# Spare expert tiles on pads, the first batch's text turned first, router logits between weight chunks, early expert tiles behind fewer scatters

## The chip, the cores and the metric

One NeuronCore of a Trainium2 chip runs the whole program as one launch. The metric is device time in microseconds (us), median of the runs; an execution taken by the hardware profiler gives the trace. Engines: TensorE (PE, its weight loads PEld), VectorE (DVE), ScalarE (ACT), GpSimd (POOL) and SyncE (SP); the last issues most DMAs.

## The reference, cut to what matters

```python
h = _L0_tok_ref(log_dt, inv_A_real, A_imag, B_ri, x, 256)      # (8, 256, 256): image tokens from a Vandermonde sum
h = jnp.concatenate([h, txt], axis=1)                          # (8, 768, 256): 256 image rows, 512 text rows
h = h + _L0_attn_ref(_layernorm(h), Wq, Wk, Wv, Wo)            # 16 heads, 4 KV heads, rotary, width 64
h = h + _L0_ffn_ref(_layernorm(h), Wr, br, W1, b1, W2, b2)     # mixture of experts

# _L0_ffn_ref, on 6144 tokens xf of width 256, 8 experts, top 2:
logits = xf @ Wr + br
topk_w, topk_idx = jax.lax.top_k(logits, 2)
topk_w = jax.nn.softmax(topk_w, axis=-1)
h_e = relu(xf @ W1[e] + b1[e]);  y_e = h_e @ W2[e] + b2[e]     # 256 -> 512 -> 256
out = sum over the two chosen e of topk_w[e] * y_e
```

Everything is f32. With the given inputs the reference sends 2973, 3193, 593, 370, 1534, 1205, 1973 and 447 token copies to experts 0 to 7 (2616 to expert 0 in the first seven batches).

## The kernel before, in words

The program has four stages, each in blocks of its own; a block starts when every engine has ended the one before.

1. `vandermonde` computes the image rows of all batches on DVE (complex products), PE (L197) and ACT (copies into `kt`, L171). SP loads all inputs at its start, ends with the stores of batch 0's image rows to `img_d` (L143) and waits for them.
2. `attention` has a start for batch 0 and then a loop of 32 iterations (8 batches x 4 KV heads), 24 steps each: PE scores (L656), DVE maximum (L812), ACT exponential (L725), DVE transpose (L818), PE values (L663). In the start SP loads `x` (batch 0: image from `img_d`, L516, text, L517), the rotary table (L612) and stores the other seven batches' image rows (L614). DVE takes the mean and variance of six 128-row tiles (`stats`), a chain of small instructions gives the reciprocal root, POOL normalises tiles 0 and 1 (L781) and DVE tiles 2 to 5 (L850). PE transposes (L633), ACT copies to `xT` (L713), PE projects K then Q in halves of 384 tokens (L642; `FIRST` is the list of these jobs), ACT copies each into `raw`, and `rotate` on DVE (L470 to L475) applies the rotary table to K half 0, K half 1, Q half 0, Q half 1, with `probT` as scratch. SP moves K (`move_k`), then the first four heads of Q (L622), and the scores start. `probT` lies where `kt` was, so DVE waits for the image stores first.
3. `route` runs over 8 batches of six tiles. PE projects each tile with `Wo` (`project`, L980: eight chunks, so 16 instructions); after tile 1 it transposes the batch before (L988), after tile 2 it computes that batch's router logits (`logits`, L996: 24 instructions with 8 output columns each), after tile 3 its counts (L1003, L1004). DVE adds the residual, normalises, picks the two experts (`choose`) and the rows of the sorted table `xs_d` (`place`); POOL scatters the rows there (L963, twelve indirect DMAs for a batch, in `scatter`). The sorted table has a region for each expert; after its last row 128 pad rows are written (L934, L1066), with a token number past the end.
4. `experts` runs 103 tiles of 128 sorted rows (`NT`), since that many can be needed. `tile_table` on DVE computes the expert (`exp_i`) and first row (`src_i`, L1209) of each tile. SP loads rows (L1258) and `W1` (L1262, 512 KB) four tiles ahead; PE transposes (L1292), goes up (L1302) and down (L1309); DVE adds the bias and gates (L1382, L1384); POOL adds the result to the output with an indirect DMA that accumulates (L1365). Add j waits for the adds j-2 and j-3, and at the first tile of an expert also for j-1 (`adds_i`). Rows whose token number is past the end are not written. Tiles past the last real one read the last real tile again with a gate of zero, and each of them also waits for the add before. SP waits for all scatters and pads (`landed`, L1267) before it loads the first rows.

The order on each engine is that of the program; nothing is planned at run time.

Of the kernel before, what the change touches and what calls it, by code (L numbers as in the profile page):

```python
# [17 lines left out]
P = 128  # L18
NB, SEQ, D = 8, 768, 256
# [15 lines left out]
NT = TOK * TOPK // P + NE - 1  # L35
DX = D + 8
# [37 lines left out]
def vandermonde(nc, sem, io, ident, img_d, wq, wk, wv, wr, br, loaded):  # L74
# [10 lines left out]
    with ExitStack() as ctx:  # L85
# [31 lines left out]
        stored = sem("v_stored")  # L117
        id_ready, known, sq_ready = sem("v_id_ready"), sem("v_known"), sem("v_sq_ready")

        with nc.Block() as block:  # L120
            @block.sync
            def _(sp):
# [15 lines left out]
                sp.dma_start(br[:], io["br"].unsqueeze(0).to_broadcast([P, NE])).then_inc(loaded, 16)  # L138

# [63 lines left out]
            def _(v):  # L203
# [77 lines left out]
                for q in range(4):  # L281
# [11 lines left out]
                    v.wait_ge(g_ready, q + 1)  # L293

# [12 lines left out]
def attention(nc, sem, io, ident, img_d, oT_d, wq, wk, wv, loaded, kt, wo, oT, wo_in, oT_in):  # L307
# [23 lines left out]
    FIRST = N_JOBS + K_JOBS + Q_JOBS + Q_JOBS  # L331
    FIRST_AT = {"n": 0, "k": 3, "q": 7, "q1": 11}
# [9 lines left out]
    ON_POOL = 2  # L342
    NORMS = 2 * TT + 15
    Q_MOVES, K_MOVES, V_MOVES, V_STORES = 4, 4, NQ, NQ
    with ExitStack() as ctx:
# [4 lines left out]
        x, st, mv = sb("a_x", [P, TT, D]), sb("a_st", [P, TT, 6]), sb("a_mv", [P, TT, 2])  # L350
        ve, y, y2 = sb("a_ve", [P, TT]), sb("a_y", [P, TT]), sb("a_y2", [P, TT])
# [19 lines left out]
        table_in, x_in, norm_dve, norm_ready = sem("a_table_in"), sem("a_x_in"), sem("a_norm_dve"), sem("a_norm_ready")  # L371
        x_done, x_out, v_in, set_ready = (sem(f"a_{n}") for n in ("x_done", "x_out", "v_in", "set_ready"))
        q_stored, v_stored, rows_stored = sem("a_q_stored"), sem("a_v_stored"), sem("a_rows_stored")
        q_first, norm_first = [sem(f"a_q_first{j}") for j in range(GH)], sem("a_norm_first")
# [137 lines left out]
        with nc.Block() as block:  # L512
            @block.sync
            def _(sp):
# [49 lines left out]
                def iteration(b, g):  # L564
                    i = b * KV + g
                    if first_it(i):
                        hold(sp, x_done, len(N_JOBS))
                        hold(sp, rows_stored, (NB - 1) * 16)
                        load(1)
# [41 lines left out]
                load(0)  # L611
# [3 lines left out]
                hold(sp, part["k"], 2 * LINKS)  # L615
                move_k(0, 0)
# [9 lines left out]
            def _(pe):  # L626
                def project(X, job, c, h, xn, g):


                    if job == "n":  # L630
# [65 lines left out]
                pe.wait_ge(norm_ready, 1)  # L696
                pe.wait_ge(norm_first, 1)
                pe.wait_ge(loaded, LOADED)
                for n, (job, c, h) in enumerate(FIRST):
                    wait(pe, x_out, len(N_JOBS) if n == len(N_JOBS) else n - NQ + 1)  # L700
# [5 lines left out]
            def _(act):  # L706
                def evacuate(X, n, job, c, h, free):
# [4 lines left out]
                    if job == "n":  # L712
# [22 lines left out]
                def copies(b, g, s):  # L735
                    for bb, gg, n, (job, c, h) in jobs_at(b, g, s):
# [3 lines left out]
                        if job == "k" and h == 0:  # L740
                            free = part["k"], bb * (2 * LINKS) + (c + 1) * LINKS
# [24 lines left out]
                for n, (job, c, h) in enumerate(FIRST):  # L766
                    free = (part["q"], (c + 1) * LINKS) if n >= FIRST_AT["q1"] and h == 0 else None
# [4 lines left out]
            def _(pool):  # L772
                scratch = [prod[:, n, :] for n in range(4)]

                def normalise(n):
                    if n > 0:
# [704 lines left out]
```

## Time and profile before

| | us |
|---|---|
| median of 3 runs | 2267.47 (2265.6 to 2272.73) |
| the profiled execution | 2265.04 |
| span of its trace | 2263.3 |
| mean granted TensorE clock | 0.959 of full speed |

| engine | busy us | share of the span |
|---|---|---|
| PE | 2047.4 | 90% |
| PEld | 1237.6 | 55% |
| DVE | 1770.0 | 78% |
| ACT | 1072.6 | 47% |
| POOL | 879.4 | 39% |

The busy shares are averages over four stages, each with another limit, so they tell little by themselves. In a stage the reader looks for the engine that never rests, and where none is, for the chain of waits. In the rows further down, the brackets at the end of a row give the idle time of that engine before the instruction and what ended it. A granted clock of 1.00 is 2.4 GHz and 0.50 is 1.2 GHz.

### The profile page before, as it was taken

How to read it: one execution, taken by the hardware profiler on the slowest of the kernel's cores; microseconds unless marked ns; L12 is line 12 of the kernel's file. 1: busy time of each engine (PE TensorE's matmuls, PEld its weight loads, DVE VectorE, ACT ScalarE, POOL GpSimd, SP SyncE). 2: the span in 40 equal slices, each digit the busy share in tenths (PEclk: the TensorE clock that was granted, in tenths of full speed). 3: DMA queues.
4: the chain of work that ended last, by engine and by line, in shares of the span. 5: the costliest groups of instructions: out<-in, count | busy, mean ns of one | idle time of the engine just before them, and what ended most of it. 6: DMA issues, size and time to landing. Idle time of an engine off the chain costs nothing. (4 is left out here: it accounts for less than half of the span.)

```text
span 2263.3 us, 59177 instructions
## 1 busy us (share of the span) xinstructions
PE 2047.4 (90%) x21098; PEld 1237.6 (55%) x21099; DVE 1770.0 (78%) x3212; ACT 1072.6 (47%) x2463; POOL 879.4 (39%) x833
## 2 busy tenths in 40 slices
PE   0369999999999999999999999997899949999997
PEld 0234444444444444444444445443588839999996
DVE  8769999999999999999999999999144544444443
ACT  2035655655556555655665565555021114444442
POOL 0023454264344542642444436221034443444443
PEclk6689999999999999999999999999899969999998
DMA  2143543634544445435444453453677648898885
GB/s 51 43 107 90 136 118 92 159 106 103 142 113 126 117 107 137 116 108 128 120 120 120 102 133 105 117 131 95 202 258 269 216 136 212 210 212 209 215 210 117
DMA packets 189542, 317.28 MB, mean 140 GB/s; under 512 B 48661, under 2 KB 127121, under 8 KB 189329
## 3 DMA queue, kind: packets, MB, share of 16 engines
q1 hardware_dynamic: 156640, 275.39, 45.1%
q0 software_dynamic: 19440, 25.83, 6.2%
q10 hardware_dynamic: 13248, 13.13, 1.7%
q8 instruction: 144, 2.36, 0.5%
q14 instruction: 70, 0.57, 0.1%
HBM read 214.75 MB, written 92.31 MB: 136 GB/s over the span
## 5 line engine op out<-in xcount | busy, mean ns | idle before, releaser
L725 ACT ACTIVATE a_prob<-ps_s,a_nmax 128x768 f32<-128x768 f32 x768 | 686.3, 898 | 578.9 <-DVE a_nmax L812 578.9
L812 DVE TENSOR_REDUCE a_nmax<-ps_s 128x1 f32<-128x768 f32 x768 | 694.1, 943 | 49.4 <-PE ps_s L656 44.2
L818 DVE STREAM_TRANSPOSE a_probT<-a_prob 128x768 f32<-128x768 f32 x768 | 700.0, 949 | 1.4 <-PE ps_o L663 1.4
L656 PE MATMUL ps_s<-a_kT,a_qT 64*128 64x384 f32 x3072 | 614.7, 514 | 54.7 <-ACT a_prob L725 50.8
L663 PE MATMUL ps_o<-a_probT,a_vrep 32*64 32x384 f32 x12288 | 561.2, 491 | 6.8 <-DVE a_probT L818 5.0
L656 PEld LDWEIGHTS ps_s<-a_kT,a_qT 64*128 64x128 f32 x3072 | 259.7, 186 | 391.5 <-ACT a_prob L725 275.3
L788 POOL TENSOR_TENSOR a_o<-a_o,a_invrow 128x1536 f32<-128x1536 f32 x32 | 110.0, 3437 | 791.0 <-ACT a_o L733 791.0
L663 PEld LDWEIGHTS ps_o<-a_probT,a_vrep 32*64 32x64 f32 x12288 | 243.6, 132 | 293.8 <-issue 129.9
L470 POOL TENSOR_TENSOR a_prod<-a_raw,a_table 128x384 f32<-128x384 f32 x304 | 294.5, 1002 | 29.1 <-DVE a_qp L475 22.1
L1365 POOL DMA_INDIRECT out_dram<-e_y,e_row_i x103 | 160.6, 1559 | 239.9 <-DMA out_dram<-e_y,e_row_i 138.6
L1302 PE MATMUL ps_r<-e_xT,e_w 128*128 128x128 f32 x1648 | 201.8, 276 | 0.0
L1309 PE MATMUL ps_r<-ew,e_hT 128*128 x824 | 194.7, 379 | 0.0
L1302 PEld LDWEIGHTS ps_r<-e_xT,e_w 128*128 128x128 f32 x1648 | 193.3, 193 | 0.1
L1340 ACT ACTIVATE e_hT<-ps_r,e_b_now 128x128 f32<-128x128 f32 x412 | 117.8, 368 | 158.9 <-PE ps_r L1302 100.0
L980 PE MATMUL ps_r<-wo,r_oT 128*128 128x256 f32 x768 | 180.9, 397 | 9.7 <-POOL base L945 9.7
L642 PE MATMUL ps_o<-a_xT,wq 128*128 128x384 f32 x512 | 185.8, 501 | 0.0
L980 PEld LDWEIGHTS ps_r<-wo,r_oT 128*128 128x128 f32 x768 | 151.5, 200 | 32.2 <-POOL base L945 10.4
L1309 PEld LDWEIGHTS ps_r<-ew,e_hT 128*128 128x128 f32 x824 | 148.8, 190 | 16.0
L963 POOL DMA_INDIRECT xs_d<-r_xn,r_idx x96 | 93.8, 977 | 150.1 <-DVE h L1078 119.1
L725 ACT ACTIVATION_READ_ACCUMULATOR a_prob<-ps_s,a_nmax 128x1 f32 x768 | 151.0, 197 | 0.0
L642 PEld LDWEIGHTS ps_o<-a_xT,wq 128*128 128x128 f32 x512 | 91.0, 189 | 88.9 <-issue 25.6
L1382 DVE TENSOR_TENSOR e_y<-ps_r,eb 128x256 f32<-128x256 f32 x103 | 43.7, 424 | 99.9 <-PE ps_r L1309 97.9
(211 smaller groups left out, 1291.5 us busy)
## 6 DMA issues: line engine op xcount, KB each, us to landing
e_w<-in_L_ffn_W_dram SPq DMA_DIRECT2D x103, 512.0 KB, 4.3
a_qT<-q_d SPq DMA_DIRECT2D x124, 384.0 KB, 8.9
a_vrep<-v_d SPq DMA_DIRECT2D x128, 192.0 KB, 3.8
a_invrow<-inv_d SPq DMA_DIRECT2D x64, 384.0 KB, 5.1
oT_d<-a_o SPq DMA_DIRECT2D x32, 768.0 KB, 3.3
r_oT<-oT_d SPq DMA_DIRECT2D x64, 384.0 KB, 8.4
q_d<-a_qp SPq DMA_DIRECT2D x31, 768.0 KB, 3.7
e_x<-xs_d SPq DMA_DIRECT2D x103, 132.0 KB, 3.6
```

The costliest lines, as they stand in the source:

```text
L470: eng.tensor_tensor(scratch[n], a, f, ALU.mult).then_inc(done, 1)
L642: last = pe.matmul(X[:, 0:HALF], w, xn[:, k, HALF * c:HALF * c + HALF], start=(k == 0), stop=(k == KC - 1))
L656: last = pe.matmul(S[:, s % 2, r, 0:HALF], qT[rows, par, 2 * hp + c, P * t:P * t + P], kT[rows, par, :], start=True, stop=True)
L663: last = pe.matmul(O[DH * c:DH * c + DH, q, 0:HALF], vrep[rows, j % NQ, j // NQ, :], keys(par, c, j, rows), start=(j == 0), stop=(j == NJ ...
L725: act.activation(prob[:, s % RING, :].rearrange("p (r k) -> p r k", r=2), S[:, s % 2, :, 0:HALF], ACT.Exp, bias=nmax[:, s % RING:s % RING ...
L812: v.tensor_reduce(nmax[:, s % RING:s % RING + 1], S[:, s % 2, :, 0:HALF], AX.XY, ALU.max, negate=True).then_inc(max_ready, 1)
L818: v.transpose(turned(par, s), prob[:, s % RING, :]).then_inc(t_ready, 1)
L980: last = pe.matmul(A[:, t % 3, 0:D], oT[:, q, c // 2, c % 2, P * t:P * t + P], wo[:, c, :], start=(c == 0), stop=(c == KV * 2 - 1))
L1302: last = pe.matmul(H[:, q, P * f:P * f + P], w1[:, n, c, P * f:P * f + P], xT[:, q, P * c:P * c + P], start=(c == 0), stop=(c == KC - 1))
L1309: last = pe.matmul(Y[:, q, 0:D], hT[:, q, P * c:P * c + P], w2[:, bass.ds(ex, 1), c, :], start=(c == 0), stop=(c == FC - 1))
L1340: last = act.activation(hT[:, q, P * f:P * f + P], H[:, q, P * f:P * f + P], ACT.Relu, bias=b1_now[:, n, f:f + 1], scale=1.0)
L1365: pool.indirect_dma_start(out=acc_d, out_offset=bass.IndirectOffsetOnAxis(ap=row_i[:, n:n + 1], axis=0), in_=y[:, n, :], in_offset=None, c ...
```

## The change

Four things are changed.

- Start of `attention`. The text of batch 0 is loaded into `x0` in `vandermonde` and normalised there on DVE, after its last product (`normalise_rows`). In `attention` SP loads the image rows alone, PE transposes the text while DVE normalises the two image tiles (`normalise_rows` again; POOL no longer takes part), then projects K half 1 (text alone), then transposes the image, then K half 0, Q half 1, Q half 0. `rotate` follows that order and uses `prod` as scratch, so the wait for the image stores comes behind the rotations. K is moved half by half.
- `route` on PE. The logits of the batch before stand between the last six weight chunks of tile 2, one row tile after each chunk. PE's wait for POOL's constants moves from its start to `counts`.
- From `route` to `experts`. A semaphore `placed` counts 1 when batch 6 is scattered and 2 when batch 7 and all pads are. `needs_i` says for the first eight tiles which of the two they wait for. SP loads rows and `W1` in turn, tile by tile. POOL waits for the stores of `h1` before its first add.
- Spare tiles. Their row in the table is no longer held at the last real tile: `src_i` is cut to the first pad row of expert 7. They read pads, write nothing, and wait for no add but j-2 and j-3.

```diff
+def normalise_rows(v, k, x, ln, tiles):
+    st, mv, ve, y, y2 = ln
+    some = slice(tiles[0], tiles[-1] + 1)
+    for t in tiles:
+        k.mark(v.bn_stats(st[:, t, :], x[:, t, :]))
+    v.wait_ge(k.sem, k.base + k.n)
+    for t in tiles:
+        k.mark(v.bn_aggr(mv[:, t, :], st[:, t, :]))
+    v.wait_ge(k.sem, k.base + k.n)
     ...
+    for t in tiles:
+        last = v.tensor_scalar(x[:, t, :], x[:, t, :], mv[:, t, 0:1], y[:, t:t + 1], ALU.subtract, ALU.mult)
+    return last
 ...
@@ vandermonde @@
+                sp.dma_start(x0[:, IT:TT, :], io["txt"][0].rearrange("(t p) d -> p t d", p=P)).then_inc(x_in, 16)
 ...
+                v.wait_ge(x_in, 16)
+                normalise_rows(v, Tally(v, text_dve), x0, ln, range(IT, TT)).then_inc(text_ready, 1)
 ...
@@ attention @@
-    FIRST = N_JOBS + K_JOBS + Q_JOBS + Q_JOBS
+    FIRST = [("text", 0, 0), ("text", 1, 0), ("k", 1, 0), ("k", 1, 1), ("image", 0, 0), ("k", 0, 0), ("k", 0, 1),
+             ("q", 1, 0), ("q", 1, 1), ("q", 0, 0), ("q", 0, 1)] + Q_JOBS
 ...
-                load(0)
+                sp.dma_start(x[:, 0:IT, :], img_d[0].rearrange("(t p) d -> p t d", p=P)).then_inc(x_in, 16)
                 sp.dma_start(table[:], io["rotary"]).then_inc(table_in, 16)
 ...
-                hold(sp, part["k"], 2 * LINKS)
-                move_k(0, 0)
+                for r in (1, 0):
+                    hold(sp, part["k"], (2 - r) * LINKS)
+                    for h in range(2):
+                        at = DH * r + HH * h
+                        sp.dma_start(kT[at:at + HH, 0, :], kp[0:HH, h, HALF * r:HALF * r + HALF]).then_inc(k_in[0], 16)
 ...
-                pe.wait_ge(norm_ready, 1)
-                pe.wait_ge(norm_first, 1)
+                pe.wait_ge(text_ready, 1)
 ...
+                    if n == IMAGE_AT:
+                        pe.wait_ge(norm_ready, 1)
 ...
-                normalise(0)
 ...
-                for at in range(6):
-                    stats(v, 0, at)
 ...
+                v.wait_ge(x_in, 32)
+                k = Tally(v, norm_dve)
+                normalise_rows(v, k, x, ln, range(IT)).then_inc(norm_ready, 1)
 ...
+                for job, c, number in (("k", 1, 0), ("k", 0, 1), ("q", 1, 0), ("q", 0, 1)):
+                    rotate(v, job, c, number, [prod[:, n, :] for n in range(4)], FIRST.index((job, c, 1)) + 1, [])
                 v.wait_ge(rows_stored, (NB - 1) * 16)
-                flat = probT[:].rearrange("p a b q -> p (a b q)")
-                for job in "kq":
-                    for c in range(2):
-                        rotate(v, job, c, c, [flat[:, HALF * n:HALF * n + HALF] for n in range(4)], FIRST_AT[job] + 2 * c + 2, [])
 ...
@@ route @@
+            if isinstance(b, int) and b >= NB - 2:
+                if b == NB - 1:
+                    for r in range(2):
+                        pool.wait_ge(zeroed[r], 16 * (NE // 2))
+                pool.nop().then_inc(placed, 1)
+            else:
+                pool.nop().then_inc(xn_free, 1)
 ...
             for c in range(KV * 2):
                 last = pe.matmul(A[:, t % 3, 0:D], oT[:, q, c // 2, c % 2, P * t:P * t + P], wo[:, c, :], start=(c == 0), stop=(c == KV * 2 - 1))
+                if beside is not None and c >= KV * 2 - TT:
+                    logits(beside, [c - (KV * 2 - TT)])
             last.then_inc(oT_free, 1)
 ...
-                if not first(b) and t == LOGITS_AT:
-                    logits(b - 1)
 ...
-        pe.wait_ge(const, 4)
 ...
+            k.link(v.tensor_scalar(full[:], off[:, 0, 0:1], 1.0 / P, -1.0, ALU.mult, ALU.add))
+            k.link(v.tensor_scalar(needs_i[:], tile_no[:, 0:AHEAD], full[:], 1.0, ALU.is_gt, ALU.add))
 ...
@@ tile_table @@
-    link(v.tensor_scalar(last[:], end[:, NE - 1:NE], -1.0, None, ALU.add))
-    link(v.tensor_scalar(jr[:], j[:], last[:], None, ALU.min))
 ...
-    link(v.tensor_scalar(ind[:], j[:], last[:], None, ALU.is_gt))
 ...
+    link(v.scalar_tensor_tensor(out=start[:], in0=e[:], scalar=float(STRIDE), in1=start[:], op0=ALU.mult, op1=ALU.add))
+    v.tensor_scalar(src_i[:], start[:], run[:, NE - 1:NE], None, ALU.min).then_inc(rows_ready, 1)
     link(v.tensor_tensor(turn[:, 1:NT], e[:, 1:NT], e[:, 0:NT - 1], ALU.is_gt))
-    link(v.tensor_tensor(turn[:, 1:NT], turn[:, 1:NT], ind[:, 1:NT], ALU.max))
 ...
@@ experts @@
+            if isinstance(j, int) and j < AHEAD:
+                needs = sp.value_load(at(needs_i, j), min_val=1, max_val=2)
+                hold(sp, placed, needs)
 ...
-        for n in range(2):
-            load_w1(n, n)
-        for s, value in landed:
-            sp.wait_ge(s, value)
         for n in range(RING):
             load(n, n)
-        for n in range(2, RING):
             load_w1(n, n)
 ...
+            if isinstance(j, int) and j == AHEAD - RING - 1:
+                sp.wait_ge(placed, 2)
 ...
         pool.wait_ge(adds_ready, 1)
+        pool.wait_ge(h_stored, 16 * NB)
```

## Rows read from the trace of the kernel before

**Rows 1.** Busy time by stage: stretch, its us, busy us of each engine, clock, DMA share, GB/s
```profile
143.50:1583.00 1439.50, 1382.36 (x15844) 644.06 (x15844) 1390.98 (x1703) 852.44 (x1853) 612.35 (x609) 1.00 0.46 118
1611.00:1818.50 207.50, 207.48 (x1048) 183.81 (x1048) 95.53 (x514) 33.18 (x50) 72.91 (x82) 0.95 0.71 236
1862.40:2248.50 386.10, 385.08 (x2674) 358.61 (x2673) 158.89 (x713) 156.81 (x514) 157.48 (x101) 1.00 0.86 205
```

**Rows 2.** Timeline of DVE, last product to first rotation: start, duration, instruction, idle before
```profile
91.84 1.22 DVE L292 TENSOR_TENSOR gim<-tm 128x1024 f32<-128x1024 f32 x1
...
108.94 2.06 DVE L496 BATCH_NORM_STATS2 a_st<-a_x 128x6 f32<-128x256 f32 x6 [15.88 <-DMA a_x<-in_txt_dram]
...
114.75 1.61 DVE L850 TENSOR_SCALAR a_x<-a_x,a_mv,a_y 128x256 f32<-128x256 f32 x4
...
127.15 1.96 DVE L470 TENSOR_TENSOR a_probT<-a_raw,a_table 128x384 f32<-128x384 f32 x4 [10.75 <-ACT a_raw L719]
```

**Rows 3.** Timelines of SP, PE and ACT in the start of attention
```profile
104.54 0.38 SPq L516 DMA_DIRECT2D a_x<-img_d  x1
...
117.50 2.82 PE L633 MATMUL ps_o<-ident,a_x 128*128 128x128 f32 x12 [17.04 <-POOL a_x L781]
121.01 8.28 PE L642 MATMUL ps_o<-a_xT,wk 128*128 128x384 f32 x16 [0.69 <-ACT a_xT L713]
...
126.53 0.49 ACT L719 ACTIVATE a_raw<-ps_o 128x384 f32<-128x384 f32 x1 [2.07 <-PE ps_o L642]
...
139.43 10.97 SPq L622 DMA_DIRECT2D a_qT<-a_qp  x16
...
143.54 2.66 PE L656 MATMUL ps_s<-a_kT,a_qT 64*128 64x384 f32 x8 [3.94 <-DMA a_qT<-a_qp]
```

**Rows 4.** Busy time in short stretches, columns as in the first group
```profile
122.00:124.00 2.00, 2.00 (x5) 1.09 (x4) 0.00 (x0) 0.03 (x1) 0.00 (x0) 0.50 0.00 0
...
160.10:163.50 3.40, 1.80 (x8) 0.60 (x8) 3.40 (x5) 1.88 (x4) 0.00 (x0) 1.00 0.56 231
...
1675.03:1678.60 3.57, 3.57 (x20) 3.16 (x19) 2.42 (x24) 0.75 (x2) 0.96 (x1) 1.00 1.07 382
...
1700.19:1705.40 5.21, 5.21 (x19) 4.29 (x19) 2.42 (x24) 1.49 (x2) 0.96 (x1) 0.67 1.08 365
```

**Rows 5.** Chain that ended last, the logits of one batch: start, us, what
```profile
1724.46 2.58 PE ps_r L996 x24
```

**Rows 6.** Timelines of POOL and PE, start of route
```profile
1610.15 0.21 POOL L940 MEMSET r_ones<- 128x128 f32 x1 [3.62 <-POOLq L512]
...
1610.97 29.87 PE L980 MATMUL ps_r<-wo,r_oT 128*128 128x256 f32 x128 [9.70 <-POOL base L945]
```

**Rows 7.** From the last scatters to the first tile: timelines, chain, and the page's DMA issues
```profile
1829.77 0.96 POOL L963 DMA_INDIRECT xs_d<-r_xn,r_idx  x1 [0.31 <-issue]
...
1847.53 0.26 DVE L1209 SCALAR_TENSOR_TENSOR src_i<-t_e,t_start 128x103 int32<-128x103 f32 x1
...
1855.25 2.43 DMA xs_d<-r_xn,r_idx
...
1858.49 3.66 SPq L1258 DMA_DIRECT2D e_x<-xs_d  x4
...
1862.39 2.70 PE ps_r L1302 x16
...
e_w<-in_L_ffn_W_dram SPq DMA_DIRECT2D x103, 512.0 KB, 4.3
```

**Rows 8.** Timelines of DVE and POOL over the last five tiles
```profile
2235.46 0.35 DVE L1384 TENSOR_SCALAR e_y<-e_y,e_gate 128x256 f32<-128x256 f32 x1
2236.76 1.55 POOL L1365 DMA_INDIRECT out_dram<-e_y,e_row_i  x1 [2.05 <-DVE e_y L1384]
...
2248.16 0.35 DVE L1384 TENSOR_SCALAR e_y<-e_y,e_gate 128x256 f32<-128x256 f32 x1
...
2255.17 1.55 POOL L1365 DMA_INDIRECT out_dram<-e_y,e_row_i  x1 [2.98 <-DMA out_dram<-e_y,e_row_i]
```

More of the change, by code:

```diff
@@ L35 @@
 NT = TOK * TOPK // P + NE - 1
+AHEAD = 8
 DX = D + 8
@@ L627, in project @@
                 def project(X, job, c, h, xn, g):
-                    if job == "n":
+                    if job == "text":
+                        for m in range(TT - IT):
+                            last = pe.transpose(X[:, P * m:P * m + P], x[:, IT + m, P * c:P * c + P], ident[:])
+                    elif job == "image":
+                        for m in range(4):
+                            last = pe.transpose(X[:, P * m:P * m + P], x[:, m % IT, P * (m // IT):P * (m // IT) + P], ident[:])
+                    elif job == "n":
                         for m in range(4):
@@ L766, in _ @@
                 for n, (job, c, h) in enumerate(FIRST):
-                    free = (part["q"], (c + 1) * LINKS) if n >= FIRST_AT["q1"] and h == 0 else None
+                    free = (part["q"], (2 - c) * LINKS) if n >= FIRST_AT["q1"] and h == 0 else None
                     evacuate(O[:, n % NQ], n, job, c, h, free)
@@ L1007, in iteration @@
             for t in range(TT):
-                project(b, q, t)
+                project(b, q, t, b - 1 if not first(b) and t == LOGITS_AT else None)
                 if not first(b) and t == TURN_AT:
                     turn(b - 1, 1 - q)
-                if not first(b) and t == LOGITS_AT:
-                    logits(b - 1)
                 if not first(b) and t == COUNTS_AT:
@@ L1184, in tile_table @@
     ni = sb("t_ni", [P, NE], I32)
-    last = sb("t_last", [P, 1])
-    jr, e, start, ind, turn = (sb(f"t_{x}", [P, NT]) for x in ("jr", "e", "start", "ind", "turn"))
+    e, start, turn = (sb(f"t_{x}", [P, NT]) for x in ("e", "start", "turn"))
     past = sb("t_past", [P, NT, NE - 1])
@@ L1446, in program @@
         with nc.Block() as block:
-            landed = route(nc, block, sb, PS, sem, io, ident, img_d, oT_d, xs_d, acc_d, oT, oT_in, wo_in, h1, run, base, exp_i, src_i, tail_i, held_by, adds_i, wo, wr, br, weights, sem("weights_in"), table_ready, adds_ready)
-            experts(nc, block, sb, PS, sem, io, ident, xs_d, acc_d, exp_i, src_i, held_by, adds_i, weights, landed, table_ready, adds_ready)
+            placed, h_stored = route(nc, block, sb, PS, sem, io, ident, img_d, oT_d, xs_d, acc_d, oT, oT_in, wo_in, h1, run, base, exp_i, src_i, tail_i, needs_i, held_by, adds_i, wo, wr, br, weights, sem("weights_in"), table_ready, adds_ready)
+            experts(nc, block, sb, PS, sem, io, ident, xs_d, acc_d, exp_i, src_i, needs_i, held_by, adds_i, weights, placed, h_stored, table_ready, adds_ready)
 def rotary_tables():
```

93 lines of the change are left out of this document (54 added, 39 removed).

## The prediction

> **What bounds the kernel now.** I read the busy time by stage first [rows 1]. Attention is bound by DVE (1390.98 us busy of 1439.5), route by PE (207.48 of 207.5) and the experts by PE (385.08 of 386.1). None of the three loops is cut by the change, so what can be won lies at their edges, where no engine is full, and in the clock of route, whose mean is 0.95. The timelines of DVE, SP, PE and ACT around the start of attention come next [rows 2, 3]: DVE rests 15.88 us for the load of `x`, then 10.75 us for the first K. Short stretches show the clock [rows 4], the chain of waits the length of a batch of route [rows 5], and the timelines the starts of route and of the experts and the end [rows 6 to 8].
>
> **Start of attention.** Before, all six tiles wait for the load; DVE works from 108.94 to 116.36 (7.42 us) [rows 2], PE starts K at 121.01, and ACT begins the copy of its second part at 126.53, 5.52 us later [rows 3]. The four rotations run back to back from 127.15 [rows 2] to the move of Q, issued from 139.43, 3.06 us each; the scores start at 143.54, 4.1 us after the last rotation [rows 3].
>
> After, the text's share of the DVE work is 7.42 less two tiles of six (statistics 2.06 / 3 = 0.7, and some 0.2 for their means), 6.5 us. It starts when the last product ends, 93.06 [rows 2], and ends near 99.6; SP leaves the old block only at 104.54 [rows 3], so it costs nothing. If that cover were gone it would cost up to 6.5 us. The text load stands last of SP's input loads, some 70 us before its use. In the new block PE starts near 104.7 with two transpose jobs. Three took from 117.50 to 121.01 with their copies [rows 3], so two take 2.6: K half 1 starts at 107.3, its second copy begins 5.52 later and ends at 113.3, and DVE can rotate from 113.4. For the two image tiles DVE needs 7.42 less four tiles' statistics and means (1.7) and half of the scaling (0.8): 4.9 us. Their 256 KB land between 106.5 and 108.9 (the last is when 768 KB had landed), so they are ready at 111.4 to 113.8: about when PE and DVE want them. The image transposes and their copy take some 1.7, so K half 0 starts at 114.7.
>
> From here the clock matters. PE ran at 0.50 from 122 to 124 [rows 4], and soon after 126.53 at the higher level: the other two K jobs took 8.28 - 5.52 = 2.76 together [rows 3]. It rose some 5.6 us after K began; the same distance from 107.3 is 112.9, just before the image transposes. A PE that rests half of the time keeps 1.00 (1.80 us busy of 3.40) [rows 4], so I take K half 0 at the higher level: copies out at 114.7 + 2.8 + 0.7 = 118.2. DVE then rotates K half 1 from 113.4 to 116.5, K half 0 from 118.3 to 121.3, Q half 1 to 124.4 and Q half 0 to 127.4: 12.0 us before 139.4. At the lower level the second copy is out 2.7 later and the gain is 9.3. I take 11.5, near the first, with something for the start of the block; 9 to 12.5 is the range. The move of Q and its 4.1 us stay. What is late next: DVE's wait for the image stores, now between rotations and loop. No byte moved from 122 to 124 [rows 4], so they are over 5 us before 127.4. K's moves stand behind SP's seven stores and before Q's; both halves are issued before 124. POOL's first rotation now waits for both Q rotations, but it must wait anyway for Q's moves, whose issues alone take 10.97 us [rows 3]. The rotary table is issued 0.4 earlier, and the first rotation has 1.8 us to spare before K half 0 is due. The loop behind is DVE's, so the shift goes through to the end: -11.5.
>
> **Route.** The logits are 24 instructions in 2.58 us, 0.107 each [rows 5]: weight loads with nothing to hide behind, since eight columns stream in no time. Between chunks there are again four such loads and the next chunk's after each pair of streaming instructions, one of the five hidden: 6 x 4 x 0.107 = 2.57. The move by itself saves nothing. But the projection behind them took 5.21 us at clock 0.67 in five of the seven batches (this row and its like) and 3.57 at 1.00 in the other two [rows 4]: after 2.58 us of hardly any streaming the engine falls to 1.2 GHz for part of the next tile. The two kinds of batch, from logits to logits, are 26.85 (1700.19 - 2.58 to 1724.46) and 25.16 long (1675.03 - 2.58 to 1700.19 - 2.58) [rows 4, 5]. Interleaved, PE streams half of the time, and half kept 1.00 in attention. So five batches become 25.16 long: -5 x 1.69 = -8.4; the short batches show that nothing else holds PE up at that pace. `choose` starts some 0.4 us later, behind the later third addition; DVE's 2.42 us in the 3.57 before the counts [rows 4] leave room for it. The first logits now need `xT` three chunks, 1.3 us, after the transposes; a copy of 384 columns takes ACT 0.49 [rows 3], so the last one, 0.6 or so for 512, should be done by then. If it is not, PE waits some tenths in each batch, within the range. PE's wait for constants took from 1610.15 to 1610.97 [rows 6]; without it I take 0.7 of 0.8 (0 to 0.8). DVE still waits for all constants, but PE needs its first addition only at the fourth tile: -0.7.
>
> **From route to the experts.** The table is ready at 1847.79 [rows 7]. It loses three small links, a 0.5 us comparison with a pointer operand twice, and gains two links of `needs_i` and one such operation: about 1847.4. Before, SP then waited for the last scatter, landed 1857.68, issued the first rows at 1858.49, and `up` of tile 0 began at 1862.39 [rows 7]. Expert 0 had 2616 rows, over 20 tiles, before the last batch, so all eight early tiles wait for batch 6 alone, whose last scatter was issued at 1829.77 [rows 7] and landed, at 2.4 as the last one of all, near 1832. SP needs 0.8 from release to issue [rows 7], and some 0.45 for one more register: rows at 1848.6, `W1` 1.15 later at 1849.8, landed after 4.3 [rows 7] at 1854.1, the second `W1` 2.7 behind. Tile 0 goes up at 1854.1 for 2.70 [rows 7], tile 1 at 1856.9 (before: 1862.39 + 2.70 + 0.22 for the transposes = 1865.31), 8.4 us earlier. The weights were hidden behind the scatters before and now stand on the path, beside scatters that run until 1857.68; I take -8.0, range 5 to 9. Later weights come 2.7 us apart against a tile of 3.73. The wait for `placed` 2 comes after tile 3's loads, with the last scatter landed; POOL's new wait and its scatters end before the first add is due, near 1862.
>
> **The end.** Experts need 24, 25, 5, 3, 12, 10, 16 and 4 tiles, 99 of 103, so four are spare, and five adds start 18.41 us from first to last, each waiting for the one before, while their rows come every 3.73 [rows 8]. Without that wait add 101 (ready at 2235.81 + 3 x 3.73 = 2247.0) starts 0.94 later, as add 98 did [rows 8], and occupies POOL for 1.55 + 0.3; add 102, ready at 2248.51, starts at 2249.8 instead of 2255.17: -5.4. From the last start to the end of the span are 8.1 us, the landing among them; nothing is written now, where 63 rows were, and I take 0.4 for that (0 to 1.5). -5.8. The Trainium skill, "DMA: Bandwidth & Descriptors", section "Anatomy of one DMA", puts most of a small DMA's fixed 2 us to the receipt of its last write; by that the empty add would land no sooner and the 0.4 would be 0, and no row here shows an empty one.
>
> **Sum.** 11.5 + 8.4 + 0.7 + 8.0 + 5.8 = 34.4 off the profiled execution's 2265.04: 2230.6. The median of the runs is 2.4 higher and the fastest run 0.6, so I add 0.9: 2231.5.
>
> **Rivals.** (1) The clock falls in route all the same, because tiny instructions in the mix still count for little: 2231.5 + 8.4 = 2240. For it: five of seven fell after 2.58 us; against it: the half-idle stretch at 1.00. 16%. (2) K half 0 runs at 1.2 GHz or DVE gets the image late: 9.3 instead of 11.5, 2234. 12%. The Trainium skill, "TensorE: Matmul & The Clock Gate", "Part 4: PE-mode transpose", says transposes do not count as PE being busy; by it the image transposes are a rest in the warming and this rival is the likelier. (3) Rows, weights and scatters share the queues, and the first tiles wait: 4 instead of 8, 2235.5. 9%. (4) The spare tiles still wait, or an empty add takes as long as a chain: the end gives nothing, 2237. 3%. (5) Slower than before: the mixed stretch counts as rest and the engine stays low for most of each batch. One fall costs 1.69; it takes 34.4 / 7 = 4.9 us in each batch, three falls in a row, to eat all gains; with four it is 2231.5 + 47.3 = 2279. Against it: a mean of 0.67 over 5.21 us means that even a fallen clock was back within that group [rows 4]. 3%. The forecast itself, within 4 us: 57%.
>
> **How the numbers follow.** The likeliest case gives 2231.5. Downwards the bounds (12.5, 9, 7) allow 5.5. Upwards cases 1 to 4 reach 2240, two together 2243; the range 2226 to 2243 leaves out case 5 and some tails. A measurement tells 0.3%, 6.8 us, from no change; all cases but the fifth are faster: 0.96, 0.01, 0.03.
>
> **What would show it.** Scores start near 132 instead of 143.5; the L980 groups after the logits all last near 3.5 us, seven batches of 25.2; `up` of tile 0 begins 8 us less after the drain of route; the last five adds are 3.7 apart or less. Wrong would be a first rotation waiting for the table, a clock under 1.00 in route's middle, or weights landing over 5 us after issue in the first tiles.

## The result, and the profile after

| | before | after |
|---|---|---|
| median of 5 runs, us | 2266.53 | 2254.49 (2249.15 to 2262.54) |
| the profiled execution | 2265.04 | 2256.40 |
| span of its trace | 2263.3 | 2254.4 |

The ratio is 0.995, with a 95% interval of 0.9937 to 0.9963: 12 us faster, where 35 were forecast. The forecast of 2231.5 and its whole range lie below it.

The trace after, cut where the terms of the sum meet, by the start of route's first projection, the first scatter of batch 7, the start of `up` of tile 2 and the end of the span:

| stretch | before | after | difference | forecast |
|---|---|---|---|---|
| to route's first projection | 1610.97 | 1594.61 | -16.4 | -12.2 (11.5 and 0.7) |
| from there to batch 7's first scatter | 229.15 | 245.56 | +16.4 | -8.4 |
| from there to `up` of tile 2 | 28.76 | 25.48 | -3.3 | -8.0 |
| from there to the end | 394.42 | 388.75 | -5.7 | -5.8 |

The start and the end did what was forecast. Route lost what the start had won. Its stretches after (us, busy time of each engine, PEclk, DMA share, GB/s): all projections, then in one batch PE's pause ahead of the logits with the first of them, the 8.54 us behind that (the rest of tile 2 with its logits), and the next 6 us.

```profile
1594.61:1818.50 223.89, 215.93 (x1048) 189.74 (x1048) 95.05 (x514) 33.40 (x50) 73.35 (x86) 0.92 0.65 219
1679.13:1681.52 2.39, 0.69 (x5) 0.69 (x5) 0.76 (x2) 2.18 (x4) 0.96 (x1) 0.94 1.07 398
1681.52:1690.06 8.54, 8.54 (x32) 7.64 (x32) 0.51 (x2) 0.68 (x1) 0.96 (x1) 0.50 1.00 339
1690.06:1696.05 5.99, 5.99 (x19) 4.87 (x19) 2.57 (x25) 1.49 (x2) 1.92 (x2) 0.60 0.12 45
```

Before, a slow projection after the logits took 5.21 us [rows 4]; here PE stands at 0.50 for 8.54 us and is still not back at 1.00 behind that. What it did before it fell is in the timeline of the same tile (start, us, engine, operation, idle time before it and what ended it):

```profile
1676.36 1.47 PE L1033 MATMUL ps_r<-ident,r_xn 128*128 128x128 f32 x12
1677.67 1.46 PE L1023 MATMUL ps_r<-wo,r_oT 128*128 128x256 f32 x6
1679.20 0.60 ACT L1079 ACTIVATE r_xT<-ps_r 128x512 f32<-128x512 f32 x1 [7.28 <-PE ps_r L1033]
1679.25 0.42 DVE L1123 TENSOR_TENSOR h<-ps_r,h 128x256 f32 x1 [3.91 <-remote]
...
1680.83 0.69 PE L1042 MATMUL ps_r<-wr,r_xT 128*128 128x8 f32 x4 [1.70 <-ACT r_xT L1079]
```

The engines wait for each other by semaphores, counters that one engine raises and another waits for. The transposes begin at 1676.36, and the first four of twelve are all that ACT's first copy needs. It begins 2.84 us later. DVE's add of tile 1, whose projection had ended when the transposes began, starts 2.89 us later. So two engines act late on two semaphores, both raised by PE, while PE's own rows go on without a gap until it reaches its wait for `xT` and idles 1.70 us. (In the text a signal is late when the engine that waits for it starts late; a trace shows that start, not when the semaphore changed.) PE idles 0.91, 1.70, 1.83, 1.75 and 1.76 us in batches 2 to 6; in batches 1 and 7 the copy starts 0.63 us behind the transposes, PE waits for nothing, and the clock stays at 1.00. From one batch's counts to the next are 26.4, 33.8, 32.2, 30.5, 27.2, 25.2 and 24.9 us. Against `interleave_alone` below, which has the same work and no late signal (projections of 199.23 us, PE never idle), the 223.89 us hold 7.96 us of idle PE and 16.7 us more of busy PE. The pause of 0.91 us in batch 2 was followed by ten microseconds at 1.00; the lower clock stands behind the longer ones.

### The profile page after: what moved, and what is told of

It is laid out like the page before. It is cut to its first block and busy times, and to the rows that moved or that the text cites. A ratio compares the mean times of both kernels' runs of the same rounds, so it can differ in the third digit from the quotient of the medians.

```text
span 2254.4 us, 59220 instructions
## 1 busy us (share of the span) xinstructions
PE 2051.4 (91%) x21098; PEld 1240.2 (55%) x21099; DVE 1771.6 (79%) x3227; ACT 1071.3 (48%) x2463; POOL 875.4 (39%) x831
## 5 line engine op out<-in xcount | busy, mean ns | idle before, releaser
L1023 PE MATMUL ps_r<-wo,r_oT 128*128 128x256 f32 x768 | 192.4, 404 | 9.1 <-DVEq L1214 9.1
```

The source lines that it names most:

```text
L1023: last = pe.matmul(A[:, t % 3, 0:D], oT[:, q, c // 2, c % 2, P * t:P * t + P], wo[:, c, :], start=(c == 0), stop=(c == KV * 2 - 1))
```

## The experiments

Eighteen runs in five sittings. A sitting is a group of up to four kernels run one after the other on one chip, each time another chip; the kernel before ran in all of them with medians of 2266.8, 2264.4, 2265.2, 2264.5 and 2263.8 us. The result above was taken apart from them, and its chip isn't on record. "Lag" is the start of ACT's first copy to `xT` behind the start of the transposes.

### First sitting: where the logits stand

Logits behind tile 2 again (`logits_behind`), between the chunks of tile 3 (`logits_tile3`), PE's loop written out (`pe_unrolled`), and two row tiles of logits behind each of the last three chunks (`logits_late`).

```diff
 logits_behind
-                project(b, q, t, b - 1 if not first(b) and t == LOGITS_AT else None)
+                project(b, q, t)
+                if not first(b) and t == LOGITS_AT:
+                    logits(b - 1, range(TT))
 logits_tile3
-    TURN_AT, LOGITS_AT, COUNTS_AT = 1, 2, 3
+    TURN_AT, LOGITS_AT, COUNTS_AT = 1, 3, 4
 ...
-                    paced = (b + 1) * TT + COUNTS_AT + 4 + t
+                    paced = (b + 1) * TT + 3 + 4 + t
 pe_unrolled
+        if eng is nc.tensor:
+            for b in range(NB):
+                iteration(b, b % 2)
 logits_late
-                if beside is not None and c >= KV * 2 - TT:
-                    logits(beside, [c - (KV * 2 - TT)])
+                if beside is not None and c >= KV * 2 - TT // 2:
+                    logits(beside, [2 * (c - (KV * 2 - TT // 2)), 2 * (c - (KV * 2 - TT // 2)) + 1])
```

> The changed kernel with the router logits put back behind the whole of tile 2; the start, the spare tiles and the boundary stay changed. Changed kernel: route takes 223.9 us for the projections against 207.5 before, PE waits 1.7 us for xT in the middle of tile 2 of the loop's batches, and the clock is near 0.50 for 6 to 14 us after that. Every theory that puts the loss on the logits between the chunks expects here: no wait for xT, route back at 207.5 with the low stretches of 3.1 us behind each group of logits, and 2238 to 2242 us. A theory that the loss came from elsewhere (the earlier start, other DMA traffic) expects route still near 224 and about 2254.

> The logits stand between the chunks of tile 3 instead of tile 2, the counts behind tile 4. Theory A (the wait for xT comes too early in the loop's batches, PE's signals to ACT are held up while it stands there, PE idles 1.7 us and the clock falls from the idle time): no wait of PE at the logits, ACT's first copy 0.5 us after the transposes begin as before, clock 1.00 through the middle of each batch, batches of 25.2 us, projections of 199 to 201 us, 2229 to 2234 us. Theory B (the mixed stretch itself lets the clock fall): clock still about 0.50 behind it, route 215 to 224, 2245 to 2254.

> The changed kernel with the route loop of PE alone written out, so that its waits are against constants; the order of its instructions is unchanged. Theory A in the form that the register wait is what holds up the signals: as in the two batches that stand outside the loop, ACT's first copy is 0.5 us after the transposes begin in every batch, PE waits at most some tenths for xT, clock 1.00 in the middle, projections near 200 us, 2229 to 2236 us. If the place of the wait alone is to blame, or ACT's and DVE's own register waits, or the DMA traffic of the loop: the copies stay 2.8 us late, PE idles 1.7 us, about 2254.

> The logits of two row tiles behind each of the last three chunks of tile 2, so PE reaches its wait three chunks (1.3 us) later; everything else as in the changed kernel. Theory A: if PE's signals are held up until it has drained the chunks before the wait, the first copy is late by 1.3 us more (about 4.1 us after the transposes begin) and PE idles 1.7 us all the same, about 2254. If PE's signals came late for another reason and only the copies' end matters, the idle time shrinks from 1.7 to 0.4 us, the clock stays up, 2232 to 2238.

| | median us | lag in batches 2 to 6 |
|---|---|---|
| `logits_behind` | 2245.86 | 3.28, 2.88, 3.47, 3.03, 2.96 |
| `logits_tile3` | 2264.29 | 3.46, 5.95, 6.15, 5.73, 6.58 (6.57 in batch 7) |
| `pe_unrolled` | 2252.49 | 2.92, 3.20, 2.92, 3.09, 2.95 (2.94 in batch 7) |
| `logits_late` | 2253.36 | 3.09, 3.06, 2.88, 3.05, 2.88 |

The theory of the held-up wait fell. `pe_unrolled` waits against constants and lags as much. In `logits_behind` PE's wait comes 2 us later, and the lag is the same:

```profile
1683.29 1.47 PE L1033 MATMUL ps_r<-ident,r_xn 128*128 128x128 f32 x12
1684.60 3.62 PE L1023 MATMUL ps_r<-wo,r_oT 128*128 128x256 f32 x16
1686.17 0.60 ACT L1081 ACTIVATE r_xT<-ps_r 128x512 f32<-128x512 f32 x1 [7.33 <-PE ps_r L1033]
1686.23 0.42 DVE L1125 TENSOR_TENSOR h<-ps_r,h 128x256 f32 x1 [3.96 <-remote]
...
1688.36 0.42 DVE L1125 TENSOR_TENSOR h<-ps_r,h 128x256 f32 x1 [1.37 <-PE ps_r L1023]
```

The last row is the add of tile 2, 5.07 us behind the transposes, as before the change (5.08): here PE itself isn't late. The whole tile 2 covers the lag in this kernel, whose projections take 207.2 us, as before (207.5). So the lag doesn't need the interleaving, which only exposes it.

Where the lag is longer, PE stops too. In batch 4 of `logits_tile3` it pauses for 1.03 us inside tile 2, ahead of the last of 16 matmuls that have no wait between them, and goes on 0.11 us before ACT starts:

```profile
1716.99 3.70 PE L1023 MATMUL ps_r<-wo,r_oT 128*128 128x256 f32 x15
...
1721.72 1.67 PE L1023 MATMUL ps_r<-wo,r_oT 128*128 128x256 f32 x7 [1.03 <-issue]
...
1721.83 0.60 ACT L1079 ACTIVATE r_xT<-ps_r 128x512 f32<-128x512 f32 x1 [10.53 <-remote]
1721.88 0.42 DVE L1123 TENSOR_TENSOR h<-ps_r,h 128x256 f32 x1 [6.94 <-remote]
```

Batch 4 of `logits_behind` has such a pause of 0.28 us, `tile3_again` of up to 0.92, and no on-time trace has one. So late signals are not all of it: for up to a microsecond PE stands still together with the two engines that wait for it.

`logits_late` was expected to recover if only the end of the copies mattered. PE's idle time did shrink, to 0.44 to 0.64 us, but nothing came back. In batch 3 the clock holds 1.00 through the pause and the logits and then stands at 0.50 for the 2.00 us from 1691.59. The logits stand twice as thick there (eight small matmuls to two large ones), so this run doesn't tell the pause from the mix.

### Second and third sitting: which part brings the lag

In the second, the kernel before with the interleaving alone (the `beside` of the change's diff), the changed kernel with PE's wait for the constants back at its start, and the kernel before with only that wait moved. In the third, the changed kernel without the wait, with it in both places, and with one or sixteen empty instructions ahead of PE's first projection.

```diff
 const_early (const_late_alone is the reverse, on the kernel before)
         def counts(b):
-            pe.wait_ge(const, 2)
 ...
+        pe.wait_ge(const, 4)
         pe.wait_ge(wo_in, 16)
 no_const: only the first of these; const_both: only the second
 nop1, nop16
         pe.wait_ge(wo_in, 16)
+        for _ in range(1):     # 16
+            pe.nop(nofuse=True)
```

> The kernel before with the interleaved logits and nothing else of the change. In the changed kernel, and also with the logits put back behind tile 2, the end of tile 1 and of the transposes reaches DVE and ACT 2.3 to 3.3 us late in batches 2 to 6 (0.3 and 0.6 us in the kernel before), so the lateness does not come from the interleaving. Theory C (another part of the change brings the lateness, the interleaving only makes PE wait for it): here DVE's add stands 0.3 and ACT's first copy 0.6 us behind the start of the transposes in all batches, PE waits 0.6 us at most, the clock is 1.00 in the middle, route's projections take 198 to 200 us against 207.5, 2256 to 2259 us. Theory D (the lateness belongs to the route itself and the kernel before was lucky, or the interleaving adds to it): copies late here too, projections 207 to 224, 2266 to 2282.

> The changed kernel with one thing undone: PE waits for the constants once at its start, as before, and no longer ahead of each batch's counts. If that wait in the loop is what makes PE's signals late in batches 2 to 6: copies 0.6 us after the transposes begin, clock 1.00 in the middle, projections 198 to 200 us, 2230 to 2236. If not: copies 2.9 us late as in the changed kernel, PE idles 1.7 us, 2254 to 2256.

> The kernel before with PE's wait for the constants moved to the counts of each batch, nothing else. If that wait makes PE's signals late: DVE's add and ACT's first copy come 2.9 us behind the start of the transposes in batches 2 to 6. If not: 0.3 and 0.6 us in all batches as before. Either way about 2266, since the whole of tile 2 covers the copies.

> The changed kernel without any wait of PE for the constants (DVE waits for them before its first instruction, and PE waits for DVE, so the wait orders nothing new). With that wait at PE's start PE's signals were on time and 19.5 us were gained over the changed kernel. Theory W (the wait in the loop makes the signals late): signals on time here, first projection 0.6 us earlier than with the wait at the start, 2234 us. Theory P (what counts is how many instructions PE's stream has ahead of its loop, and the wait at the start shifts it by one; the wait in the loop is innocent, as it was in the kernel before): late here as well, since nothing stands at the start, 2252 to 2256.

> The changed kernel with the wait for the constants at PE's start as well as ahead of each batch's counts. Theory W (the wait in the loop makes PE's signals late): late by 2.3 us in batches 2 to 6, about 2254. Theory P (the place of the stream's instructions): on time in every batch, 2232 to 2238.

> The changed kernel with one empty instruction ahead of PE's first projection; the waits are unchanged. Theory W: late, about 2254. Theory P: if the one more instruction at the start is what helped, on time in every batch, 2232 to 2238.

> The same with sixteen empty instructions. Theory W: late, about 2254. Theory P: on time or late according to where the loop comes to lie; if both this and the run with one empty instruction are late, P is out in this form.

| | median us | lag in all batches |
|---|---|---|
| `interleave_alone` | 2256.67, ratio 0.9969 (0.9958 to 0.9979) | 0.63 |
| `const_early` | 2234.95, ratio 0.9867 | 0.63 |
| `const_late_alone` | 2265.53 (one run) | 0.63 |
| `no_const` | 2234.32, ratio 0.9862 | 0.63 |
| `const_both`, `nop1`, `nop16` | 2236.16, 2234.80, 2230.78 (one run each) | 0.63 |

After the second sitting the wait for the constants looked guilty. The third has it absent, doubled and untouched, with 0, 1 or 16 more instructions, and none lags. No property of the code that was varied divides the kernels that lag from those that don't; the sitting does. `interleave_alone` is the clean price of the interleaving without the lag: seven batches of 25.1 to 25.3 us from logits to logits, projections of 199.2 us against 207.5, 7.8 us between the medians.

### Fourth sitting: the changed kernel itself, and the boundary

`after_again` is the changed kernel without an edit. `all_scatters_first` and `w1_on_act` build on `no_const`: the first rows behind all scatters, and the first four loads of `W1` issued by ACT.

```diff
 all_scatters_first
-                needs = sp.value_load(at(needs_i, j), min_val=1, max_val=2)
-                hold(sp, placed, needs)
+                sp.wait_ge(placed, 2)
 w1_on_act
         for n in range(RING):
             load(n, n)
-            load_w1(n, n)
 ...
+        act.wait_ge(table_ready, 1)
+        for n in range(RING):
+            ex = act.value_load(at(exp_i, n), min_val=0, max_val=NE - 1)
+            act.dma_start(w1[:, n], ...).then_inc(w1_in[n], 16)
         copy_x(0, 0)
```

> The changed kernel once more, unchanged, beside the same kernel without the wait. One removed wait and one added empty instruction each put PE's signals on time, which no theory of the code explains; all late runs (the changed kernel and the four variants with the logits elsewhere or PE's loop written out) came from two sittings, all on-time runs from two others. Theory J (the lateness belongs to the sitting, the chip or its hour, and the code is innocent): on time here with 2232 to 2237 us, or late here and in the kernel without the wait too. Theory C (the code decides, by the wait in the loop together with the place of the stream): late here, 2252 to 2256, and the kernel without the wait on time.

> The changed kernel without PE's wait for the constants, a second time, in the same sitting as the unchanged one. Theory J: the same as that one, within 0.15%, on time or late together. Theory C: on time, 2233 to 2236, with the unchanged one 18 to 20 us longer.

> Without PE's wait for the constants and with the first row loads behind all scatters and pads (no table of needs), to price the boundary by itself. My prediction gave the boundary 8.0 us, the changed kernel showed 3.4 and the on-time run without the wait 4.9. If the early loads are worth what the on-time trace shows, 4.9 us more than without the wait's kernel, 2239. If the scatters that run beside slow SP's steps and the weights down, part of it comes back through 0.35 us steps: 2 to 3 us more.

> Without PE's wait for the constants, and the first four W1 loads issued by ACT instead of SP. SP issues the rows of tile j+1 2.4 to 3.8 us behind those of tile j there, because the reads of the tables and two DMAs stand on one engine. If SP's steps bound the first tiles: all four rows and weights are issued within 5 us, up(0) 1 us and up(3) 3 us earlier, 2231. If the transfers of W1 beside the scatters bound them (2.7 us each): at most 1 us less, 2233 to 2235.

| | median us | ratio |
|---|---|---|
| `after_again` | 2232.34 (2231.40 to 2233.02) | 0.9859 (0.9842 to 0.9875) |
| `no_const_again` | 2232.90 | 0.9861 (0.9845 to 0.9878) |
| `all_scatters_first` | 2243.00 | 0.9905 (0.9889 to 0.9922) |
| `w1_on_act` | 2236.65 | 0.9876 (0.9859 to 0.9892) |

The unchanged code takes 2232.3 us here, 22 less than in the result, with a lag of 0.63 us in every batch it shows. The first theory of the code fell with it. The same tile as above, in `after_again`:

```profile
1677.36 1.47 PE L1033 MATMUL ps_r<-ident,r_xn 128*128 128x128 f32 x12
1677.67 0.42 DVE L1123 TENSOR_TENSOR h<-ps_r,h 128x256 f32 x1 [1.33 <-PE ps_r L1023]
1677.99 1.57 ACT L1079 ACTIVATE r_xT<-ps_r 128x512 f32<-128x512 f32 x3 [5.08 <-PE ps_r L1033]
...
1678.66 1.46 PE L1023 MATMUL ps_r<-wo,r_oT 128*128 128x256 f32 x6
...
1679.96 0.51 PE L1042 MATMUL ps_r<-wr,r_xT 128*128 128x8 f32 x4
```

The copies end at 1679.56, and PE passes its wait without a pause at 1679.96. The stretches: all projections, two across the logits, and the tiles behind them.

```profile
1596.83:1796.32 199.49, 199.49 (x1048) 177.90 (x1048) 95.32 (x514) 33.19 (x50) 73.24 (x86) 0.99 0.74 246
1678.00:1683.40 5.40, 5.40 (x38) 5.07 (x37) 0.43 (x2) 2.85 (x4) 2.96 (x4) 1.00 1.07 399
1683.40:1687.20 3.80, 3.80 (x24) 3.44 (x23) 2.20 (x21) 0.00 (x0) 1.03 (x2) 1.00 1.06 395
1687.20:1701.20 14.00, 14.00 (x68) 12.30 (x67) 9.75 (x50) 1.70 (x3) 6.65 (x7) 1.00 0.67 191
```

The boundary is worth 10.1 us (`no_const_again` against `all_scatters_first`; expected were 4.9, or 2 to 3 more), more than against the kernel before, which had loaded two `W1` under the scatters while this variant loads none. `w1_on_act` was expected at 2231, or at 2233 to 2235, and is 3.8 us slower than `no_const_again`: ACT issues its `W1` loads from 1827.40, ahead of the first rows or between them, and the first rows are turned 4.7 us after their issue (1828.54 to 1833.26) instead of 2.6 (1826.94 to 1829.53). That the weights hold up the rows is the likely reason, not a tested one.

### Fifth sitting: is it one of two levels

> The changed kernel a third time, in a new sitting. So far one sitting each gave 2254.5 with PE's signals 2.3 us late in batches 2 to 6, and 2232.3 with them on time. If the lateness belongs to the chip or the sitting: either 2231 to 2236 with ACT's first copy 0.63 us behind the start of the transposes, or 2250 to 2258 with 2.9 us; nothing between.

> The logits back behind the whole of tile 2, in the same sitting. Where signals are on time the interleaving is worth what it gave alone, 8.1 us in the trace: 2240 to 2242, 8 us over the changed kernel. Where they are late, the order turns round: 2246, 8 us under it.

> The logits between the chunks of tile 3, in the same sitting. Where signals are on time: PE waits for nothing at the logits, and the counts behind tile 4 leave DVE's placing 1 us ahead of tile 5's end, so projections of 199 to 200 us and the time of the changed kernel, 2232 to 2234. Where they are late: DVE and ACT get the signal only 3.5 to 6 us behind the transposes, as before, and about 2264.

| | median us | ratio | lag in batches 1 to 7 |
|---|---|---|---|
| `after_third` | 2250.84 (2244.92 to 2256.01) | 0.9933 (0.9911 to 0.9956) | 0.64, 0.63, 3.04, 2.83, 2.83, 0.63, 3.22 |
| `behind_again` | 2244.96 | 0.9913 (0.9896 to 0.9931) | 0.64, 2.97, 1.11, 2.67, 1.86, 2.75, 0.64 |
| `tile3_again` | 2277.21 (2273.11 to 2284.51) | 1.0069 (1.0045 to 1.0094) | 0.64, 3.30, 5.91, 6.50, 7.98, 5.15, 2.87 |

The lag is back in all three kernels. The changed kernel comes near its first result. The levels aren't exactly two: here some batches lag and some don't, and the changed kernel spreads over 11 us where it spread over 1.6 on time. With the lag, interleaving loses 5.9 us; without it, alone, it gains 7.8. Tile 3, which was to free PE of its wait, is the worst place: in batch 4 ACT's copy comes 6.50 us and DVE's add 6.54 us behind the transposes, in batch 5 the copy 7.98 and the add 3.87, and in this sitting the kernel is slower than the kernel before. Tile 3 never ran on time, so its worth there is open, and so is whether the wait for the constants matters where there is a lag.

### What the lag is

In all eight traces that have it, it shows in route from batch 2 on and at the first loads of the experts. In batch 1 the scatters haven't begun, and no trace shows it there. The attention loop takes 1464.7 to 1469.4 us in the lagging traces and 1465.2 to 1470.0 in the on-time ones with the same start. It isn't the DMA load. The 2.84 us behind the start of those transposes in the trace after and in `after_again`, and the lag of batch 7 in `pe_unrolled`, in this order:

```profile
1676.36:1679.20 2.84, 2.77 (x19) 2.26 (x17) 0.00 (x0) 0.00 (x1) 1.68 (x2) 1.00 1.07 392
```

```profile
1677.36:1680.20 2.84, 2.84 (x22) 2.69 (x21) 0.76 (x2) 1.61 (x4) 2.23 (x3) 1.00 1.06 397
```

```profile
1794.67:1797.61 2.94, 2.77 (x19) 2.26 (x17) 0.06 (x1) 0.00 (x1) 1.75 (x2) 1.00 0.25 92
```

The same load comes with and without the lag, and the lag with a quarter of it, where little but POOL's scatters was moving; batch 7 of `after_third` is alike (3.22 us at a share of 0.28). Nor does a fetch of instructions stand behind it: between 1670 and 1800 the trace after shows no packet in its instruction queues, and four of its lags lie there. At the boundary SP's own instructions are slow in the same sittings. SP's queue in the trace after, and then in `after_again`:

```profile
1849.02 0.38 SPq L1305 DMA_DIRECT2D e_x<-xs_d  x1
1850.49 0.41 SPq L1309 DMA_DIRECT2D e_w<-in_L_ffn_W_dram  x1
...
1853.87 0.70 SPq L1305 DMA_DIRECT2D e_x<-xs_d  x1
...
1857.46 0.00 SPq L1309 DMA_DIRECT2D e_w<-in_L_ffn_W_dram  x1
```

```profile
1826.94 0.37 SPq L1305 DMA_DIRECT2D e_x<-xs_d  x1
...
1828.41 0.41 SPq L1309 DMA_DIRECT2D e_w<-in_L_ffn_W_dram  x1
...
1830.21 0.34 SPq L1305 DMA_DIRECT2D e_x<-xs_d  x1
...
1831.62 0.38 SPq L1309 DMA_DIRECT2D e_w<-in_L_ffn_W_dram  x1
```

From the rows of tile 1 to its `W1` take 3.59 us in the first and 1.41 in the second; in six other traces of the lagging sittings 2.10 to 4.33 and in the eighth, `tile3_again`, 1.52; in the other on-time ones with this order of loads 1.39 to 1.42. From the rows of tile 0 to those of tile 1 take 4.12 to 5.45 in all eight and 3.26 to 3.28 in those on time. So in these stretches several engines make small steps late together. Whether the signals leave late, travel late or are acted on late, no trace tells. Whether the chip or the hour brings it wasn't settled either: none of the five sittings shared a chip. And every kernel traced in a lagging sitting had the other parts of the change; the trace of the kernel before is from none of the five and `interleave_alone` ran in an on-time one alone, so whether they lag there is open.

## Why the prediction was wrong

**Start of attention: right.** Forecast scores at 132 and 12.2 us less to route, the constants included. The trace after has 129.78. Over the fifteen traces with this start and without PE's early wait the scores start at 128.7 to 132.1 (141.7 to 143.5 with the old start) and route at 1593.5 to 1601.0, mean 1598.0, against 1611.0 to 1611.5 in the three traces with the old start, mean 1611.2: 13.2. The 16.4 of the first table is near one end of that scatter and so in part luck; the attention loop alone varies by 4.8 us. K half 0 ran at the higher clock: its two copies begin at 114.58 and 115.87, and the rotations of both K halves at 112.46 and 116.46. The rival with the cold K, for which the Trainium skill ("TensorE: Matmul & The Clock Gate", "Part 4: PE-mode transpose") spoke because by that section transposes don't count in the same way as PE being busy, didn't occur in this trace: behind the image transposes the clock was up.

**Route: the mechanism right, one step failed.** That half-streaming PE keeps its clock, and that five batches shrink to 25.16, is what `interleave_alone` and all on-time traces show: 7.9 to 8.3 us in the projections, 8.4 forecast. The step that failed is "the last one should be done by then. If it is not, PE waits some tenths in each batch". It took PE's signal to ACT at the few tenths that the one trace of before shows and bounded only the copy. In the trace after the first copy comes 1.5 to 3.0 us behind the start of the transposes in batches 2 to 6 instead of 0.63, and PE waits 0.9 to 1.8 us; behind the longer waits the clock is lower, and a tile that takes 3.57 us at 1.00 took 6.14 (from 1689.91 in the trace after). Rival 1 named the outcome (the clock falls all the same, 8.4 lost) with another cause and half the size, rival 5 the size of a batch but not the mechanism. The loss was 16.4 where 8.4 were to be gained; that alone carries the forecast from 2231.5 past its range.

**Constants: right.** PE idles 9.68 to 9.70 us ahead of route's first projection in the four traces that wait for the constants there and 9.03 to 9.14 in the sixteen that don't: 0.6 us against 0.7 forecast, too little to see in a median.

**Route to the experts: mis-sized.** Forecast 8.0; 3.3 in the trace after, 5.6 in `after_again`. Three steps were short. In `after_again` SP takes 1.84 us from the table to the first issue (1825.10 to 1826.94), not 0.8 and 0.45. The first `W1` follows 1.47 behind the rows, not 1.15. And PE turns tile 1 ahead of `up` of tile 0, which the sum left out: the first `W1` has landed at 1832.59, but PE turns tile 1 only at 1833.70, for rows issued at 1830.21, and `up` of tile 0 starts at 1834.19 behind it. With the lag these rows are issued 4.85 us behind the first ones instead of 3.27, and it came to 3.3. That was rival 3 in size ("4 instead of 8"), by SP's pace and the order on PE rather than by full queues.

**The end: right.** 5.7 and 5.4 us against 5.8. The last five adds after start 3.74, 3.73, 3.71 and 1.87 us apart, and the last no longer waits for the one before to land:

```profile
2233.52 1.55 POOL L1409 DMA_INDIRECT out_dram<-e_y,e_row_i  x1 [1.72 <-DMA out_dram<-e_y,e_row_i]
2237.26 1.56 POOL L1409 DMA_INDIRECT out_dram<-e_y,e_row_i  x1 [2.18 <-DMA out_dram<-e_y,e_row_i]
2240.99 1.55 POOL L1409 DMA_INDIRECT out_dram<-e_y,e_row_i  x1 [2.18 <-DVE e_y L1429]
2244.70 1.56 POOL L1409 DMA_INDIRECT out_dram<-e_y,e_row_i  x1 [2.16 <-issue]
2246.57 1.56 POOL L1409 DMA_INDIRECT out_dram<-e_y,e_row_i  x1 [0.30 <-issue]
```

From the last start to the end of the span are 7.87 us in each of the seventeen traces with this end, and 8.07 to 8.17 in the three with the old one: the empty write is worth 0.2 to 0.3 of the 0.4 forecast. The prediction read the Trainium skill, "DMA: Bandwidth & Descriptors", "Anatomy of one DMA", as making it nothing; the traces show a little more than that.

**The sum.** In `after_again` the four stretches give 14.1, 7.9, 5.6 and 5.4, together 33.1 off the span, 34.4 forecast, and its median is 0.8 us over the 2231.5. That it comes so close is in part luck: the start gave 1.9 more than forecast and the boundary 2.4 less, and the kernel before was 2 us faster in that sitting than in the result's (32.2 us between the medians, 35.0 forecast). The forecast holds where the signals are on time and is 19 to 23 us short where they aren't. The range's lower end doesn't follow from its bounds: 12.5, 9 and 7 against 11.5, 8.0 and 5.8 allow 3.2 us, not 5.5.

## What to carry to other kernels

A wait that doesn't show in the profile is covered by the work that stands between the signal and the wait. When a change shortens this cover, price the signal as well as the work, and against more than one execution. Here a move that leaves 1.3 us of cover gains 8 us in one sitting and loses 6 in another, since PE pays for the wait and then for its clock. A version meant for any chip would keep the logits behind tile 2 (2245 to 2246 in two lagging sittings, and some 2240 on time, an estimate from 2232.3 and 7.8). More cover by tile 3 didn't help: the lag grew with it. When a result contradicts a sound sum, run the unchanged kernel again, in another sitting, beside the first experiments: eleven runs here looked for a cause in the code.

## What the runs showed of the hardware

- ACT and DVE started 0.2 to 0.6 us behind PE's work in three sittings and up to 3.5 us (6.5 with the logits in tile 3) in three others, the result's among them, with the same code and the same DMA share (1.07 and 1.06). PE went on at full rate for 3 to 5 us behind the start of the transposes and then, in three traces, stopped too, for 0.3 to 1.0 us.
- The lag also stands at a DMA share of 0.25 (92 GB/s), and where no instruction packet moves.
- In the same sittings SP needed 4.1 to 5.5 us between the rows of the first two tiles, a step that otherwise takes 3.3.
- A pause of 1.70 us in PE was followed by 8.54 us at a granted clock of 0.50, one of 0.91 us by 10 us at 1.00; a mixed stretch of chunks and tiny matmuls, 5.40 us without a pause, kept 1.00.
- An accumulating DMA whose rows are all past the end left 7.87 us to the end of the span in seventeen traces, one with 63 rows 8.07 to 8.17 in three.
- Route was reached up to 7.5 us apart by fifteen traces whose code is the same up to there.
